# Key and value projections as seven block products instead of eight, with rotation and splitting moved into attention

## Chip, cores and metric

One core of a Trainium2 chip. The metric is the device time of one execution in microseconds, lower is better. Kernels are compared by runs on the same chip.

## What is computed

Two layers of a gated cross-attention model over 8 sequences of 256 tokens (2048 tokens in all, 1024 features), all in float32:

```
x = x + tanh(g_xattn[0]) * autocorrelation(layernorm(x), ctx, ctx)
x = x + tanh(g_ffn[0])   * lora_ffn(layernorm(x))
x = x + tanh(g_xattn[1]) * gqa_attention(layernorm(x), ctx, ctx, mask, wq, wk, wv, wo)
x = x + tanh(g_ffn[1])   * fourier_ffn(layernorm(x))
```

The change is about the keys and values of the third line: `k = rope(ctx @ wk)` and `v = ctx @ wv`, both 2048x1024 by 1024x1024, with 8 heads of 128 for the 32 query heads. `rope` turns each head: `x*cos + rot*sin`, where `rot` exchanges the two halves of the 128 dimensions.

## The kernel before

Each large product is done as three products of parts: a float32 matrix is split into a high part (a copy rounded to fp32r, on ScalarE) and a low part (the rest, a subtraction on VectorE or GpSimd), and `three` (L147 to L152) adds high x high, high x low and low x high into one PSUM bank. So every matmul needs both parts of both operands in SBUF.

The stages run in a chain on each engine, in an order that is written out by hand: each stage has one generator per engine, and `weave` (L3132) decides at which yields the next stage's pieces are put between. The stages: kv (keys and values, L194 to L528), ac (autocorrelation, L532), f0 (first FFN), qp (queries, already as seven products), at (attention, L2274), wf (factors of the last FFN's weight, spread into attention) and f1 (last FFN). Waits are semaphores by name and key (`on.wait_ge(*at(...))`); each engine works its list in order.

**kv.** The weights wv and wk are loaded, split and kept whole in SBUF. Tokens come in four blocks `tb` of 512; a block's 8 chunks of `ctxT` (128 features x 512 tokens) are split into `kv_ch`, `kv_cl`. An output tile (128x512) is 8 chunks x 3 matmuls into one bank; there are 32 tiles of values and 32 of keys. A tile of values leaves PSUM by a ScalarE copy and a VectorE subtraction, both stored to `vd[0]`, `vd[1]`; a tile of keys is turned by three VectorE products out of PSUM (L389 to L391), added and split on GpSimd (L432, L434) and stored to `kd[0]`, `kd[1]`. The last 8 tiles of values are done one by one, and `weave` puts the first pieces of ac between them: two tiles, then two pieces of ac, and so on (L3136 to L3140).

**ac's first pieces.** Piece 1 issues the loads of the tables, x and ctx. Pieces 2 and 3: `table(0)` (L690, L844), the split of the first context, `stats(0)` (L849), `normalise(0)` and the split of the first query, whose low part is on VectorE (L943). Pieces 4 and 5: the other tables and, on TensorE, the first `spectra(0)` and `odd_spectra(0)` (L579, L597). Piece 6: `correlate(0)`.

**at.** 128 steps `u`, each: transposes of the weights of step u-2, scores of step u, values of u-2, and the output product; four steps share one head group's 512 keys and values. `load_kv` (L2604) brings high and low parts of keys and values ready to use, four DMAs at every fourth step (u%4 == 2), into two buffers.

Of the kernel before, what the change touches and what calls it, by code (L numbers as in the profile page):

```python
# [162 lines left out]
def flamingo(nc, x, ctx, ctxT, mask, gates, w0T, b0, agT, bT, gb, wq, wk, wv, wo,  # L163
             w1T, b1, enc, coef, cmask, tab, four, rope, ident, out):
    es = ExitStack()
    with es:
# [5 lines left out]
        kd = [nc.dram_tensor(f"kd{i}", [G, P, T], F, kind="Internal").ap() for i in range(2)]  # L172
        w1d = nc.dram_tensor("w1d", [D, D], F, kind="Internal").ap()
        w1f = nc.dram_tensor("w1f", [7, P, 2, 4, 512], F, kind="Internal").ap()
        vd = [nc.dram_tensor(f"vd{i}", [T, D], F, kind="Internal").ap() for i in range(2)]
# [18 lines left out]
        kv_wvh = [place(f"kv_wvh{i}", 32 * i, [P, C, 512], R) for i in range(2)]  # L194
        kv_wvl = [place(f"kv_wvl{i}", 32 * i + 16, [P, C, 512], R) for i in range(2)]
        kv_ch, kv_cl = place("kv_ch", 64, [P, C, 512], R), place("kv_cl", 80, [P, C, 512], R)
        kv_oh, kv_ol = place("kv_oh", 96, [P, 4, 512], R), place("kv_ol", 104, [P, 4, 512], R)
        kv_wkh, kv_wkl = place("kv_wkh", 112, [P, C, D], R), place("kv_wkl", 144, [P, C, D], R)
        kv_rc = place("kv_rc", 176, [P, 8, 512])
        kv_t1, kv_t2 = place("kv_t1", 192, [P, 2, 512]), place("kv_t2", 196, [P, 2, 512])  # L200
        kv_rt = place("kv_rt", 200, [P, 2, 512])


        KV_OUT = [("v", 0, i) for i in range(8)]
        for tb in range(4):
            KV_OUT += [("k", tb, g) for g in range(G)]
            if tb in (1, 2):
                KV_OUT += [("v", tb, i) for i in range(8)]
        KV_OUT += [("v", 3, 2 * tt + hf) for hf in range(2) for tt in range(4)]
        KV_NO = {o: n for n, o in enumerate(KV_OUT)}  # L210
        KV_SRC = [(wv, c) for c in range(C)] + [(wk, c) for c in range(C)]

        def kv_high(i, hf):
            c = i % C
            return kv_wvh[hf][:, c, :] if i < C else kv_wkh[:, c, halves(hf)]

        def kv_low(i, hf):
            c = i % C
            return kv_wvl[hf][:, c, :] if i < C else kv_wkl[:, c, halves(hf)]

        def kv_slot(i, hf):
            return 4 + 2 * (i % 2) + hf

        def kv_bank(o):
            kind, tb, i = o
            return i if kind == "k" or tb < 3 else 4 + (i // 2) % 2

        def kv_renews(tb, c):

            return "kv_pool" if tb == 0 or c % 3 == 2 else "kv_dve"  # L230
# [3017 lines left out]
```

## Time and profile before

| | |
|---|---|
| three runs | 2989.80, 2990.52, 2991.84 us; median 2990.52 |
| profiled execution, first to last instruction | 2990.3 us (its span; no other time of it is given) |
| TensorE busy | 2959.3 us, 99% |
| VectorE, ScalarE, GpSimd busy | 2009.8, 1282.8, 1369.9 us |
| mean granted TensorE clock | 0.998 of 2.4 GHz |

The share of busy time is a mean over stages with different limits; a matmul's printed duration overlaps with the next one's, so TensorE's pace is read from the distance between starts.

### The profile page before, as it was taken

To read this page: it belongs to the slowest core of one execution; us is meant where nothing else is said; L and a number is where in the kernel's file an instruction comes from. 1 tells how busy PE (TensorE), PEld (TensorE's weight loads), DVE (VectorE), ACT (ScalarE), POOL (GpSimd) and SP (SyncE) were. 2 spreads that over 40 slices of the span, in tenths; PEclk is the share of its full clock that TensorE was granted. 3 is DMA by queue.
4 is the path that set the end of the run, shared out by engine and by line. 5 is a ranking of instruction groups with operands and counts; after the bars stand their busy time and mean duration, and the time that the engine had idled before them with its cause. 6 is when DMAs were issued, how large, how long until landed. Compare 5 with 4: busy or idle time off the path is not lost.

```text
span 2990.3 us, 41114 instructions
## 1 busy us (share of the span) xinstructions
PE 2959.3 (99%) x14701; PEld 2482.3 (83%) x14701; DVE 2009.8 (67%) x4714; ACT 1282.8 (43%) x2686; POOL 1369.9 (46%) x1105
## 2 busy tenths in 40 slices
PE   9999999999999999999999999999999999999999
PEld 7888878887788878887888888888888888888887
DVE  4432478888655686679667777666776676666566
ACT  4111366665422422232223666555555545544332
POOL 2422388886422587777776334322322211111264
PEclk9999999999999999999999999999999999999999
DMA  7332421212555564455444787676677666665531
GB/s 254 127 120 99 166 70 50 78 64 75 191 177 166 197 179 113 113 149 152 109 112 120 242 268 239 227 242 209 193 221 244 189 196 204 208 194 166 225 108 76
DMA packets 320661, 488.29 MB, mean 163 GB/s; under 512 B 26236, under 2 KB 155644, under 8 KB 317644
## 3 DMA queue, kind: packets, MB, share of 16 engines
q1 hardware_dynamic: 319740, 484.23, 51.0%
q8 instruction: 118, 1.93, 0.3%
q10 hardware_dynamic: 720, 1.44, 0.1%
q14 instruction: 83, 0.68, 0.1%
HBM read 324.12 MB, written 161.48 MB: 162 GB/s over the span
## 4 chain that ended last, share of the span: by engine, by line
PE 61%; DVE 3%; DMA 0%; issue 0%; POOL 0%; ACT 0%; SPq 0%; DVEq 0%; ACTq 0%
PE PB L150 19%; PE PB L151 19%; PE PB L152 19%; PE PB L2401 4%; DVE qp_b L2150 1%; PE PB L2830 0%; DVE PB L2192 0%; DMA qp_raw<-in_wq 0%; DVE qp_r L2198 0%; DVE PB L2174 0%; DVE qp_c L2194 0%; DVE qp_r L2188 0%; DVE qp_r L2189 0%; POOL f1x L3046 0%; DMA qp_in<-xod 0%
## 5 line engine op out<-in xcount | busy, mean ns | idle before, releaser
L2567 POOL TENSOR_TENSOR at_ql<-at_qf,at_qh 128x512 fp32r<-128x512 f32 x128 | 166.2, 1299 | 833.9 <-ACT at_qh L2441 833.9
L2448 ACT ACTIVATE at_ss<-at_ss,at_sm,at_bs 128x256 f32<-128x256 f32 x512 | 301.9, 591 | 317.1 <-DVE at_sm L2528 317.1
L150 PE MATMUL PB<-at_woh,at_ah 128*128 128x512 f32 x1024 | 400.4, 391 | 0.6 <-DVE at_al L2550 0.6
L151 PE MATMUL PB<-at_wol,at_ah 128*128 128x512 f32 x1024 | 399.9, 390 | 0.0
L152 PE MATMUL PB<-at_woh,at_al 128*128 128x512 f32 x1024 | 399.5, 390 | 0.0
L2558 DVE SCALAR_TENSOR_TENSOR at_xt<-PB,gt,at_xt 128x512 f32<-128x512 f32 x256 | 192.1, 750 | 249.7 <-PE PB L152 249.5
L150 PE MATMUL PB<-qp_b,qp_a 128*128 128x512 f32 x896 | 350.2, 391 | 8.4 <-DVE qp_r L2196 3.8
L151 PE MATMUL PB<-qp_b,qp_a 128*128 128x512 f32 x896 | 349.3, 390 | 0.0
L152 PE MATMUL PB<-qp_b,qp_a 128*128 128x512 f32 x896 | 349.2, 390 | 0.0
L2220 POOL TENSOR_TENSOR qp_a<-qp_raw,qp_a 128x512 fp32r<-128x512 f32 x192 | 260.0, 1364 | 101.2 <-ACT qp_a L2112 98.5
L2112 ACT ACTIVATE qp_a<-qp_raw 128x512 fp32r<-128x512 f32 x192 | 113.5, 625 | 292.1 <-POOL qp_raw L2224 162.4
L2460 ACT ACTIVATE at_pth<-PB 128x512 fp32r<-128x512 f32 x256 | 139.2, 596 | 225.0 <-PE PB L2401 225.0
L152 PEld LDWEIGHTS PB<-at_woh,at_al 128*128 128x128 f32 x1024 | 192.3, 188 | 41.0
L150 PEld LDWEIGHTS PB<-at_woh,at_ah 128*128 128x128 f32 x1024 | 192.7, 188 | 37.5 <-ACT at_ah L2471 0.8
L151 PEld LDWEIGHTS PB<-at_wol,at_ah 128*128 128x128 f32 x1024 | 192.7, 188 | 35.3
L150 PEld LDWEIGHTS PB<-qp_b,qp_a 128*128 128x128 f32 x896 | 168.5, 188 | 45.9 <-DVE qp_r L2196 4.9
L152 PEld LDWEIGHTS PB<-qp_b,qp_a 128*128 128x128 f32 x896 | 168.6, 188 | 35.5
L151 PEld LDWEIGHTS PB<-qp_b,qp_a 128*128 128x128 f32 x896 | 168.6, 188 | 34.6
L2544 DVE TENSOR_TENSOR at_ptl<-PB,at_pth 128x512 fp32r<-128x512 f32 x256 | 164.8, 686 | 40.5 <-ACT at_pth L2460 40.5
L2524 DVE CUSTOM_DVE_ANT_0 at_ss<-PB,at_bi 128x256 f32<-128x256 f32 x512 | 185.4, 418 | 0.2
L150 PE MATMUL PB<-at_kh,at_qh 128*128 128x256 f32 x512 | 154.8, 302 | 0.0
L2538 DVE TENSOR_SCALAR at_ss<-at_ss,at_sm 128x256 f32<-128x256 f32 x512 | 149.3, 356 | 4.5
(314 smaller groups left out, 7570.6 us busy)
## 6 DMA issues: line engine op xcount, KB each, us to landing
at_woh<-wod SPq DMA_DIRECT2D x48, 1024.0 KB, 7.4
at_wol<-wod SPq DMA_DIRECT2D x48, 1024.0 KB, 9.6
qp_raw<-in_wq SPq DMA_DIRECT2D x32, 1024.0 KB, 5.4
qd<-qp_r SPq DMA_DIRECT2D x256, 128.0 KB, 2.5
at_qf<-qd SPq DMA_DIRECT2D x128, 256.0 KB, 3.4
at_rawo<-in_wo SPq DMA_DIRECT2D x32, 512.0 KB, 5.3
wod<-at_woh SPq DMA_DIRECT2D x16, 1024.0 KB, 5.5
wod<-at_wol SPq DMA_DIRECT2D x16, 1024.0 KB, 6.3
```

Of the source, the lines that this page charges most:

```text
L150: pe.matmul(o, ah, bh, start=start, stop=False)
L151: pe.matmul(o, ah, bl, start=False, stop=False)
L152: return pe.matmul(o, al, bh, start=False, stop=stop)
L2220: pool.tensor_tensor(qp_part(pair, i, 1), qp_weight(pair, i), asf(qp_part(pair, i, 0)), ALU.subtract).then_inc(*inc("qp_pool", ("w", pair, ...
L2401: m = pe.transpose(PB[1][:, 512 * k + P * c:512 * k + P * c + P], at_ss[s][:, c, P * k:P * k + P], idt[:, :])
L2448: m = act.activation(at_ss[s][:, c, :], at_ss[s][:, c, :], ACT.Exp, bias=z[:, 4 + c:5 + c], scale=at_bs[:, qn % 2, 8 + 2 * b + c % 2:9 + 2 ...
L2460: self.act.activation(at_pth[:, k, :], BK[2 + k], ACT.Copy).then_inc(*inc("at_act", ("pt", u, k)))
L2524: dve.tensor_tensor_reduce(out=at_ss[s][:, c, :], in0=PB[0][:, L * c:L * c + L], in1=at_bi[qn % 2][:, 2 * b + c % 2, :], scale=1.0, scalar ...
L2538: dve.tensor_scalar(at_ss[s][:, c, :], at_ss[s][:, c, :], z[:, 12 + c:13 + c], None, ALU.mult).then_inc(*inc("at_dve", ("weight", u, c)))
L2544: self.dve.tensor_tensor(at_ptl[:, k, :], BK[2 + k], asf(at_pth[:, k, :]), ALU.subtract).then_inc(*inc("at_dve", ("pt", u, k)))
L2558: self.dve.scalar_tensor_tensor(out=xt, in0=BK[6 + p % 2], scalar=gt[:, 2:3], in1=xt, op0=ALU.mult, op1=ALU.add).then_inc(*inc("at_dve", ( ...
L2567: self.pool.tensor_tensor(at_ql[n % 3][:, :], at_qf[n % 2][:, :], asf(at_qh[n % 3][:, :]), ALU.subtract).then_inc(*inc("at_pool", ("q", n)))
```

## The change

1. **Seven products in place of eight.** The job is cut into four passes: values of the first 1024 tokens, keys of the first 1024, keys of the last 1024, values of the last 1024. In each pass the 1024x1024 by 1024x1024 product is taken as 2x2 blocks of 512, and Winograd's form gives it in seven block products `n`, in the order of `KV_SEQ`. A block product is 4 tiles x 4 chunks x 3 matmuls. The seven left factors are a11, S2, S3, S1, a12, a22, S4 and the right ones b11, T2, T3, T1, b21, T4, b22 (keys swap the sides for TensorE); S1 to S4 and T1 to T4 are sums of blocks, made chunk by chunk (128x512).
2. **Operands.** Blocks are loaded again for each pass. Each chunk of each factor is split into a ring of 10 slots a side, six chunks ahead of TensorE: highs on ScalarE, lows of b (and of a's chunk 3) on VectorE, lows of a's chunks 0 to 2 on GpSimd. S1, S2, S4 are on GpSimd, S3 and all T on VectorE.
3. **Banks.** A product goes chunk by chunk over four banks, products alternating between the two sets of four; the last two go tile by tile over two banks, and ac's pieces are put between those and the product before them.
4. **Leaving PSUM.** Sums of products are formed on VectorE (ScalarE for products 0 and 2 of a pass, one GpSimd addition after product 3), and one float32 copy of keys and of values is stored, keys not turned.
5. **Attention.** `load_kv` brings keys straight and with halves exchanged, and values, in float32. GpSimd multiplies by cosine and sine (`turn_k`, at u%4 == 2), VectorE joins (`join_k`, u%4 == 3), ScalarE and GpSimd split keys and values (u%4 == 3), for the group that begins at the next step.

ac's buffers move to other addresses, and its first loads wait for the blocks that lay there (`kv_spent`).

```diff
-        KV_OUT = [("v", 0, i) for i in range(8)]
...
+        KV_SEQ = (0, 4, 3, 1, 6, 2, 5)
+        KV_PASSES = (("v", 0), ("k", 0), ("k", 1), ("v", 1))
+        KV_N = 7 * len(KV_PASSES)
+        KV_RING = 10
...
+        def kv_low(side, c):
+            return "kv_dve" if side == "b" or c == 3 else "kv_pool"
+
+        def kv_bank(n, t):
+            return 4 + t % 2 if n >= KV_N - 2 else 4 * (n % 2) + t
...
+        def kv_schedule(do):
+            do.begin()
+            for q in range(6):
+                do.prepare(q // 4, q % 4)
+            for n in range(KV_N):
+                do.product(n)
+                for t in range(4):
+                    if 4 * n + 6 + t < 4 * KV_N:
+                        do.prepare(n + 1 + (2 + t) // 4, (2 + t) % 4)
+                    do.tile(n, t)
+                    do.leave(n, t)
+                    do.load(n, t)
+                    if n >= KV_N - 2 and t % 2 and (n, t) != (KV_N - 1, 3):
+                        yield
+                if KV_N - 5 < n < KV_N - 2:
+                    yield
...
+        class KvTensor(Keys):
...
+            def chunk(self, n, t, c):
+                on, ts = self.on, slice(P * t, P * t + P)
+                for side in ("a", "b"):
+                    on.wait_ge(*at("kv_act", (side, n, c)))
+                    on.wait_ge(*at(kv_low(side, c), (side, n, c)))
...
+        class KvScalar(Keys):
...
+            def prepare(self, n, c):
...
+                    if 4 * n + c >= KV_RING:
+                        on.wait_ge(*at(*kv_chunk_done(4 * n + c - KV_RING)))
+                    self.act.activation(kv_part(side, n, c, 0), kv_factor(side, n, c), ACT.Copy).then_inc(*inc("kv_act", (side, n, c)))
...
+        class KvVector(Keys):
...
+            def prepare(self, n, c):
+                dve, on, p, k = self.dve, self.on, n // 7, n % 7
+                if n == 2:
+                    self.first_sums(0, c)
+                self.low("b", n, c)
+                if kv_low("a", c) == "kv_dve":
+                    self.low("a", n, c)
+                if k == 1 and p:
+                    self.first_sums(p, c)
...
+                if k == 2:
+                    on.wait_ge(*at(*kv_loaded("b22", p, c)))
...
+                    dve.tensor_tensor(b11, b22, t1, ALU.subtract).then_inc(*inc("kv_dve", ("T2", p, c)))
...
+            def leave(self, n, t):
...
+                if k in (0, 2):
                     return
...
+                if k == 5:
+                    dve.tensor_tensor(f, f, bank, ALU.add)
+                    m = dve.tensor_tensor(u, u, bank, ALU.add)
...
+        class KvGpsimd(Keys):
...
+            def prepare(self, n, c):
...
+                if n == 2:
+                    self.first_sum(0, c)
+                if kv_low("a", c) == "kv_pool":
...
+                    pool.tensor_tensor(kv_part("a", n, c, 1), kv_factor("a", n, c), asf(kv_part("a", n, c, 0)), ALU.subtract).then_inc(
+                        *inc("kv_pool", ("a", n, c)))
+                if k == 1 and p:
+                    self.first_sum(p, c)
...
+        class KvSync(Keys):
...
+            def begin(self):
+                for c in range(4):
+                    self.fetch("b11", 0, c)
+                for c in range(4):
+                    self.fetch("a12", 0, c)
+                    self.fetch("b21", 0, c)
+                for c in range(4):
+                    self.fetch("b12", 0, c)
+                    self.fetch("a21", 0, c)
+                    self.fetch("a22", 0, c)
+                for c in range(4):
+                    self.fetch("b22", 0, c)
...
             for u in range(NU + 5):
...
+                n = u // 4 + 1
+                if u % 4 == 3 and n < NG:
+                    do.join_k(n)
+                    do.split_k(n)
...
+                if u % 4 == 2 and n < NG:
+                    do.turn_k(n)
...
+                if u % 4 == 3 and n < NG:
+                    do.split_v(n)
                 do.split_wo(u)
...
+            def join_k(self, n):
+                dve, on, kr, ks = self.dve, self.on, at_kr[n % 2], at_ks[n % 2]
+                on.wait_ge(*at("at_pool", ("sine", n)))
+                dve.tensor_tensor(kr[0:64, :, :], kr[0:64, :, :], ks[0:64, :, :], ALU.subtract).then_inc(*inc("at_dve", ("turned", n, 0)))
+                dve.tensor_tensor(kr[64:P, :, :], kr[64:P, :, :], ks[64:P, :, :], ALU.add).then_inc(*inc("at_dve", ("turned", n, 1)))
...
+            def turn_k(self, n):
...
+                on.wait_ge(*at(f"at_k{n % 2}", ("swapped", n, 1)))
+                pool.tensor_tensor(kr[:, :, :], kr[:, :, :], c, ALU.mult).then_inc(*inc("at_pool", ("cosine", n)))
+                pool.tensor_tensor(ks[:, :, :], ks[:, :, :], s, ALU.mult).then_inc(*inc("at_pool", ("sine", n)))
...
             next(kv)
             next(ac)
-            for beside in (2, 2, 1):
-                next(kv)
-                next(kv)
-                for _ in range(beside):
-                    next(ac)
+            next(kv)
+            next(ac)
+            next(ac)
+            next(kv)
+            next(ac)
+            next(ac)
+            next(kv)
+            next(kv)
+            next(ac)
             for _ in kv:
                 pass
```

## Rows read from the trace of the kernel before

**Rows 1.** The page, part 1: busy time, share, instructions.
```profile
PE 2959.3 (99%) x14701; PEld 2482.3 (83%) x14701; DVE 2009.8 (67%) x4714; ACT 1282.8 (43%) x2686; POOL 1369.9 (46%) x1105
```
**Rows 2.** Windows of the kv stage: busy of each engine, PEclk, DMA share, GB/s.
```profile
0.00:10.00 10.00, 7.39 (x18) 3.86 (x18) 3.14 (x4) 4.36 (x7) 3.34 (x7) 1.00 0.77 238
10.00:20.00 10.00, 9.97 (x44) 8.25 (x45) 5.44 (x8) 6.45 (x12) 4.11 (x4) 1.00 0.85 282
...
50.00:60.00 10.00, 10.00 (x46) 8.29 (x45) 4.74 (x7) 2.40 (x4) 0.81 (x1) 1.00 1.01 356
...
20.00:312.00 292.00, 292.00 (x1290) 241.80 (x1289) 108.24 (x158) 62.96 (x103) 91.21 (x71) 1.00 0.40 140
```
**Rows 3.** Groups by line and shape, 0 to 367 us: busy, mean ns, idle before.
```profile
L150 PE MATMUL PB<-kv_ch,kv_wkh 128*128 128x512 f32 x256 | 99.6, 389 | 0.0
...
L432 POOL TENSOR_TENSOR kv_t<-kv_t,kv_t 128x512 f32<-128x512 f32 x32 | 41.3, 1290 | 103.9 <-DVE kv_t L391 103.9
...
L330 ACT ACTIVATE kv_oh<-kv_t 128x512 fp32r<-128x512 f32 x32 | 20.2, 632 | 137.6 <-POOL kv_t L432 137.6
...
L404 DVE TENSOR_TENSOR kv_wkl<-kv_rc,kv_wkh 128x512 fp32r<-128x512 f32 x16 | 10.9, 693 | 8.3 <-ACT kv_wkh L350 8.2
```
**Rows 4.** Timeline of PE, one tile of values: start, duration; 24 matmuls apart.
```profile
312.10 0.39 PE L150 MATMUL PB<-kv_wvh,kv_ch 128*128 128x512 f32 x1
...
317.54 0.39 PE L150 MATMUL PB<-kv_wvh,kv_ch 128*128 128x512 f32 x1
```
**Rows 5.** Timeline of the first microseconds, POOL and PE.
```profile
6.44 1.29 POOL L441 TENSOR_TENSOR kv_cl<-kv_rc,kv_ch 128x512 fp32r<-128x512 f32 x1 [5.20 <-ACT kv_ch L346]
...
7.03 2.06 PE L298 MATMUL PB<-kv_wvh,kv_ch 128*128 128x512 f32 x8 [1.30 <-ACT kv_wvh L350]
```
**Rows 6.** L2194 by operands (ns min/median/max), then timeline of DVE and POOL, queries.
```profile
L2194 DVE TENSOR_TENSOR PB<-PB,qp_rope x54: 698/699/700, 1061.4 to 1611.0; 128x512 f32<-128x512 f32 x54
L2194 DVE TENSOR_TENSOR qp_c<-qp_c,qp_rope x10: 691/1638/1661, 1071.4 to 1755.1; 128x512 f32<-128x512 f32 x10
...
1067.06 1.29 DVE L2174 TENSOR_TENSOR PB<-qp_c,PB 128x512 f32<-128x512 f32 x2
...
1069.57 1.80 DVE L2192 TENSOR_TENSOR PB<-qp_c,qp_rope 128x512 f32<-128x512 f32 x1
1071.41 1.65 DVE L2194 TENSOR_TENSOR qp_c<-qp_c,qp_rope 128x512 f32<-128x512 f32 x1
...
1073.58 1.18 DVE L2198 TENSOR_TENSOR qp_r<-qp_r,qp_c 128x512 f32<-128x512 f32 x1
...
1069.52 2.99 POOL L2220 TENSOR_TENSOR qp_a<-qp_raw,qp_a 128x512 fp32r<-128x512 f32 x2
...
1075.87 1.28 POOL L2220 TENSOR_TENSOR qp_a<-qp_raw,qp_a 128x512 fp32r<-128x512 f32 x1
```
**Rows 7.** Timeline at the handover to ac: DVE, ACT, PE.
```profile
324.55 0.96 DVE L847 TENSOR_TENSOR ac_tl<-ac_tr,ac_th 128x768 fp32r<-128x768 f32 x1
...
334.52 1.23 DVE L943 TENSOR_TENSOR ac_ql<-ac_xn,ac_qh 128x1024 fp32r<-128x1024 f32 x1 [6.18 <-ACT ac_qh L710]
...
336.86 2.95 DVE L847 TENSOR_TENSOR ac_tl<-ac_tr,ac_th 128x1024 fp32r<-128x1024 f32 x3
...
326.57 1.06 ACT L718 ACTIVATE ac_ch<-ac_cb 128x1024 fp32r<-128x1024 f32 x1 [2.06 <-DMA ac_cb<-in_ctx]
...
333.86 0.39 PE L150 MATMUL PB<-ac_ch,ac_th 128*128 128x512 f32 x1
```
**Rows 8.** Timeline of two attention steps, PE and ACT; landing times of the keys.
```profile
1805.95 0.36 PE L150 MATMUL PB<-at_kh,at_qh 128*128 128x256 f32 x1
...
1815.09 0.36 PE L150 MATMUL PB<-at_kh,at_qh 128*128 128x256 f32 x1
...
1820.82 0.61 ACT L2441 ACTIVATE at_qh<-at_qf 128x512 fp32r<-128x512 f32 x1
...
DMA to landing us min/median/max: 3.7/4.6/9.6
```

More of the change, by code:

```diff
@@ L211, in flamingo @@
[L211 to L226, printed above, removed]
@@ new lines, in kv_emptied, with kv_chunk_done @@
+        def kv_emptied(n, t):
+            return ("kv_act" if n % 7 in (0, 2) else "kv_dve", ("out", n, t))
+        def kv_chunk_done(q):
+            return ("kv_pe", ("out", q // 4, 3) if q % 4 == 3 else ("chunk", q // 4, q % 4))
+        def kv_schedule(do):
[14 more added lines that the diff above has]
+                    yield
@@ new lines, in flamingo, with none, __init__, claim @@
+        class Keys:
+            def none(self, *args):
+                pass
+            begin = prepare = product = tile = leave = load = none
+        class KvTensor(Keys):
+            def __init__(self, pe, on, spare):
+                self.pe, self.on, self.spare = pe, on, spare
+            def claim(self, n, t):
+                for e in self.spare[kv_bank(n, t)]:
+                    self.on.wait_ge(*at(*e))
+                self.spare[kv_bank(n, t)] = [kv_emptied(n, t)]
+            def begin(self):
+                self.on.wait_ge(*at("kv_pool", "zeros"))
+                for _ in range(3):
+                    self.pe.matmul(BK[0], kv_st[0][:, 0:P], kv_st[0][:, :], start=True, stop=True)
+            def chunk(self, n, t, c):
[3 more added lines that the diff above has]
+                    on.wait_ge(*at(kv_low(side, c), (side, n, c)))
+                rows, cols = ("a", "b") if KV_PASSES[n // 7][0] == "v" else ("b", "a")
+                m = three(self.pe, BK[kv_bank(n, t)], (kv_part(rows, n, c, 0)[:, ts], kv_part(rows, n, c, 1)[:, ts]),
+                          (kv_part(cols, n, c, 0), kv_part(cols, n, c, 1)), c == 0, c == 3)
+                if c == 3:
+                    m.then_inc(*inc("kv_pe", ("out", n, t)))
+                elif t == 3:
+                    m.then_inc(*inc("kv_pe", ("chunk", n, c)))
+            def product(self, n):
+                if n < KV_N - 2:
+                    for c in range(4):
+                        for t in range(4):
+                            if c == 0:
+                                self.claim(n, t)
+                            self.chunk(n, t, c)
+            def tile(self, n, t):
+                if n > KV_N - 3:
+                    self.claim(n, t)
+                    for c in range(4):
+                        self.chunk(n, t, c)
@@ new lines, in flamingo, with kv_spent @@
+        VALUES_DONE = (KV_N - 1, 3)
+        def kv_all_kept(on):
+            for t in range(4):
+                on.wait_ge(*at(f"kv_s{t}", (len(KV_PASSES) - 1, 6)))
+        def kv_spent(on, name):
+            n = KV_N - 7 + {"a11": 3, "b11": 3, "a12": 4, "b22": 4, "a21": 5, "b12": 5, "a22": 6, "b21": 6, "s1": 2, "t1": 2}[name]
+            side = "a" if name in ("s1", "a11", "a12", "a21", "a22") else "b"
+            on.wait_ge(*at("kv_act", (side, n, 3)))
+            for c in (2, 3):
+                on.wait_ge(*at(kv_low(side, c), (side, n, c)))
@@ L2317, in at_schedule @@
                 do.bias(0, part)
+            do.turn_k(0)
             yield
+            do.join_k(0)
             for n in range(2):
```

548 lines of the change are left out of this document (233 added, 315 removed).

## The prediction

> **What bounds the kernel now.** I read the page first: TensorE is busy 99% of the span, no other engine over 67% [rows 1]. So matmuls taken away shorten the run, unless something else then sets the pace of the stage they leave. The windows put that to the stage: from 20 to 312 us TensorE is busy for all of the 292 us, with VectorE busy 37% of it, GpSimd 31%, ScalarE 22%, the clock at 1.00 [rows 2]. The kv stage is bound by TensorE and by nothing else; only its first 10 us have gaps. The groups by line give prices, with the matmul's printed 389 ns overlapping the next one [rows 3]; the distance between starts is the pace: 5.44 us for 24 matmuls of 512 columns, 0.2267 us each [rows 4].
>
> **What goes.** Before: 64 tiles x 8 chunks x 3 = 1536 matmuls, 348.2 us. After: 28 products x 4 tiles x 4 chunks x 3 = 1344, 304.7 us. The shape is the same, so **43.5 us** go. A product is 48 matmuls, 10.9 us; a pass of seven 76.2 us. What VectorE, ScalarE and GpSimd did for the turned keys and the splits of the results goes too, and costs nothing, since it lay under TensorE.
>
> **What comes in the kv stage.** Per pass, in instructions on 128x512 [prices: rows 3]:
> - ScalarE: 56 highs and 8 copies out of PSUM, 64 x 0.63 = 40 us of 76. Hidden.
> - GpSimd: 21 lows, 12 sums, 4 additions: 37 x 1.29 = 48 us.
> - VectorE: 35 lows and 20 sums with both inputs in SBUF, 24 additions with one input in PSUM. Two in a row take 1.29 us, so 0.60 each [rows 6]: 33 + 14.4 = 47 us.
> - DMA: 8 MB in and 4 MB out in 76 us, some 165 GB/s, where 356 have run [rows 2]. SyncE's loads for the next pass wait for the last split of the block they overwrite and stand behind stores that wait for VectorE, but come one to four products (11 to 44 us) before their use. Hidden, but for the start.
>
> Each alone has room. But VectorE and GpSimd get in each other's way: the same line takes 699 ns at most with an input in PSUM, and 1638 in the median with both in SBUF while GpSimd works [rows 6]. Four GpSimd operations (1069.52 to 1075.87, 6.35 us) let three such VectorE ones through, so one GpSimd operation holds the inputs' way for (6.35 - 3 x 0.60) / 4 = 1.13 us. A pass needs 37 x 1.13 + 55 x 0.60 = **74.8 us** of it, 1.4 less than TensorE's 76.2. The 24 additions out of PSUM fit beside GpSimd's work or add up to 14.4 us: between 74.8 and 89.2.
>
> By product, what is prepared in the seven steps of a pass takes 14.5, 13.3, 11.1, 12.1, 6.4, 6.4 and 11.1 us of this, against 10.9 us each. Four heavy steps run late by about 7 us together, two light ones make it up. Preparation is six chunks ahead (16 us of TensorE) and VectorE's first heavy step has no PSUM addition that holds it back, so walking the queue by these prices TensorE is kept fed, by some 3 us. I take 2 us lost in each of the last three passes, **6** (bounds 0, and 3 x 13 = 39 where no addition finds cover).
>
> The Trainium skill, page "SBUF — State Buffer", section "Who interferes with whom", speaks against the change here: a VectorE instruction with two SBUF inputs and a GpSimd one share a port, and the one that comes second blocks for the first one's whole instruction. With the whole printed lengths a pass would need 37 x 1.29 + 55 x 0.69 = 86 us of the port, 10 over TensorE. The blocking is as the trace shows it; the length is not, since a GpSimd operation and a VectorE one got through in 1.73 us together, not in 1.98.
>
> **The first pass.** TensorE now waits for both lows of chunk 0: GpSimd's ends at 7.7 where TensorE began at 7.03 [rows 5]: 0.7. Product 2 needs S1, T1 and, behind them in VectorE's list, T2, which waits for b22, the last of 32 loads. Its chunk 0 is load 29, 7.6 MB. After 10 us 2.4 MB are in; at 282 to 356 GB/s the rest takes 15 to 18 [rows 2], so VectorE stands until 25 to 28. Then each chunk needs four VectorE operations, a ScalarE copy and three GpSimd ones, 5 us and up to 6.4 in strict turn (4 x 0.60 + 0.63 + 3 x 1.13), and TensorE takes 2.7. It wants the last chunk of product 2 at 37.7 and gets it at about 40 to 44. I take 4 there, 2 more for product 3, with the 0.7 **7** (3 to 11).
>
> **The handover to ac.** Before, 10.9 us of kv tiles lay between the place of pieces 2 and 3 and `spectra(0)`; now two tiles of 2.72, 5.4 us. VectorE's chain there, `table(0)` at 324.55 to the first query's low part at 335.75, took 11.2 us, of which some 2 were a late load of the context (ScalarE waited 2.06 for it); the low part was ready 0.8 us before TensorE wanted it, 12 matmuls into `spectra(0)` [rows 7]. After: VectorE comes to `table(0)` behind the additions of product 25, the last of which waits for that product's end E, so at E + 0.7 to 3; the query is ready at E + 10 to 14, TensorE wants it at E + 8.2: 2 to 6 lost. Then VectorE has three lows and four additions (7 x 0.60) ahead of `table(1)` (1.2 of the 2.95 for tables 1 to 3), which TensorE wants 2.7 later: 2.7 more. I take **7** (4 to 9). ScalarE and GpSimd have less to do there.
>
> **Attention.** Per four steps (36.6 us): ScalarE 2 x 0.63, VectorE 2 x 0.69, GpSimd 4 x 1.29, one load of 0.25 MB fewer. The chain that counts is at u%4 == 3: scores at 1815.09, exponentials done at 1820.82, 5.73 later; then the split of keys, 0.63 on ScalarE and 1.29 on GpSimd, 7.7; the next scores come 9.14 after the last [rows 8]. So 1.4 us are left, if GpSimd is free. `turn_k` waits for the loads (4.6 us in the median, 9.6 at most) a step earlier; the latest would push it into VectorE's queue. `join_k` sits in a gap before the next PSUM addition. I take **3** for all 31 groups and for the pieces put into the end of the queries (bounds 0, and 31 x 2 = 62).
>
> **Sum.** 2990.3 - 43.5 + 7 + 6 + 7 + 3 = **2970 us**. The span read stands 0.2 below the median of the runs, so nothing is added. Own range 2958 to 2980. Less than 0.2%, 6 us, counts as no change.
>
> **Rivals.**
> - **Nothing new waits** (0.17): the queues hide all but the start and half of the handover. 2990.3 - 43.5 + 3 + 4 = 2951. For it: every engine has room on average. Against: the handover's chain stands in the trace and its cover is halved.
> - **The shared port sets the pace of the passes, partly** (0.16): half the PSUM additions find no cover, 82 us a pass, 4 x 5.8 = 23 lost in the passes: 2990.3 - 43.5 + 23 + 1 + 7 + 3 = 2981, and up to 2990 at 84.4 us a pass. For it: 98% use of the port by two queues that each wait in order.
> - **It sets the pace fully, slower** (0.06): no addition is covered, 89.2 a pass, 52 lost; 2990 - 43.5 + 52 + 1 + 7 + 3 = 3010. It decides from 84.5 us a pass on, where less than a third of the additions is covered. Against it: the 1.13 us measured and that GpSimd, when the port is short, always has something to do beside an addition. By the rule of the Trainium skill's page "SBUF — State Buffer" quoted above, with whole lengths and full cover, the time would be 2996.
> - **Attention waits for keys, slower** (0.05): GpSimd's four operations come in the way of the weight factors' ones and VectorE's join waits for them; 2 us for each of 31 groups, 3029. It decides from 1 us a group on. Against: the 1.4 us of room.
>
> That it does not do what it says is out: the loops give 1344 matmuls. Forecast 0.56. Faster by over 0.2%: forecast, first rival and half of the second, 0.81; within 0.2%: the rest of the second and a little of the slow ones, 0.09; slower 0.10. The range 2952 to 2988 leaves out the two slow cases and parts of the fast one and the port's.
>
> **What would show it.** TensorE's kv matmuls 1344, at 0.2267 apart in the passes; a few us of idle in 30 to 55 us behind lows and sums; passes 76 to 79 us apart; VectorE subtractions well over 0.69 in the mean; two gaps in `spectra(0)` of 2 to 6 us, ended by VectorE; scores of every fourth step without a wait. Wrong if passes are 82 us or more apart, if the first scores of a group wait for `at_kl`, or if no gap shows at the handover.

## Result: 3038.5 us, 1.6% slower, and the profile after

The changed kernel takes **3038.47 us** (median of 4 runs, 3035.38 to 3041.25), the kernel before 2990.66 beside it: ratio 1.0158, 95% interval 1.0143 to 1.0172. The forecast was 2970, the range 2952 to 2988. The profiled execution took 3041.25 us, its span is 3039.3.

The page of the changed kernel, busy time, share and instructions, answers to [rows 1]:

```profile
PE 2950.1 (97%) x14509; PEld 2465.5 (81%) x14509; DVE 2264.7 (75%) x4916; ACT 1381.3 (45%) x2878; POOL 1675.7 (55%) x1303
```

TensorE has 89 us of gaps now where it had 31. Where they opened is read from five starts on TensorE in both traces:

| start of | before | after | difference |
|---|---|---|---|
| first transposes of ac | 376.09 | 369.24 | -6.9 |
| scores of attention's step 0 | 1617.02 | 1614.75 | -2.3 |
| scores of step 36 | 1943.05 | 1976.74 | +33.7 |
| scores of step 124 | 2747.37 | 2796.57 | +49.2 |
| end of the span | 2990.3 | 3039.3 | +49.0 |

So two things went wrong, of different weight. Of the 43.5 us of matmuls taken away, 36.6 were given back by the first transposes of ac; and attention lost 51.5 from its step 0 on, of which 36.0 in its first 36 steps. Another 4.6 went between the first transposes and step 0, most of it in one wait of 3.4 for the first group's keys (`at_kl` below), which are turned, joined and split at the end of the queries.

What TensorE waited for, the view of waits (total us, times, longest) of the changed kernel:

```profile
PE PB L150 <- POOL at_wol L2635: 17.5, 8, 2.8
PE PB L2426 <- DVE at_ss L2580: 14.9, 14, 2.0
PE PB L150 <- DVE kv_st L397: 7.6, 5, 2.4
PE PB L150 <- DVE ac_ql L954: 5.5, 1, 5.5
...
PE PB L150 <- DVE kv_a L345: 4.1, 1, 4.1
PE PB L150 <- POOL at_kl L2622: 3.4, 1, 3.4
```

The two largest are attention's, and neither is by name a wait for keys: the low part of wo, split by GpSimd, and the weights, scaled by VectorE.

**The kv stage and the handover.** TensorE's timeline, rows with a wait and the first ones behind the wait at 44:

```profile
44.28 0.77 PE L150 MATMUL PB<-kv_b,kv_a 128*128 128x512 f32 x1 [4.07 <-DVE kv_a L345]
44.84 0.63 PE L151 MATMUL PB<-kv_b,kv_a 128*128 128x512 f32 x1
45.27 0.63 PE L152 MATMUL PB<-kv_b,kv_a 128*128 128x512 f32 x1
...
49.42 0.39 PE L150 MATMUL PB<-kv_b,kv_a 128*128 128x512 f32 x1
...
133.13 0.50 PE L150 MATMUL PB<-kv_a,kv_b 128*128 128x512 f32 x1 [2.40 <-DVE kv_st L397]
...
292.27 0.79 PE L150 MATMUL PB<-kv_b,kv_a 128*128 128x512 f32 x1 [2.39 <-DVE kv_st L397]
...
322.93 0.47 PE L150 MATMUL PB<-ac_ch,ac_th 128*128 128x512 f32 x1 [2.30 <-DVE ac_tl L858]
...
331.44 0.77 PE L150 MATMUL PB<-ac_qh,ac_th 128*128 128x512 f32 x1 [5.50 <-DVE ac_ql L954]
```

A pause can cost more than its length: behind the 4.07 us matmuls start 0.43 apart instead of 0.2267 until 49.42. The windows of the same stretch show the granted clock (the number behind POOL's busy time): 0.66 in the ten us of the pause, 1.00 ahead of it.

```profile
30.00:40.00 10.00, 10.00 (x46) 8.11 (x44) 9.90 (x9) 1.69 (x3) 8.72 (x6) 1.00 0.02 9
40.00:50.00 10.00, 5.93 (x16) 4.57 (x16) 9.90 (x10) 7.95 (x18) 9.31 (x6) 0.66 0.12 45
```

Summing every distance between starts above 0.2267 gives the bill with the half clock in it: some 3 us at the start (first matmul at 8.54 instead of 7.03), 8.6 between 40 and 54, then 5.1, 1.3 and 6.4 in the three later passes, 11.9 between 320 and 339. Some 11 us of it are half clock, by the distances behind the pauses.

Not every pause has it behind it. The pause of 2.40 at 133.13 cost 4.3 us here; in the run called weights first below, with the same kv code and the same pause (at 133.29), it cost 2.7, without any half clock. In the eight traces of this kv code (the change, kv alone, no turn, turn last, keys early, one join, weights first, two moves) the first transposes begin between 366.6 and 372.4 us: the waits are alike there, the half clock is not.

Why the bank is late, in VectorE's and GpSimd's rows of the same pause:

```profile
129.04 0.67 DVE L397 TENSOR_TENSOR kv_st<-kv_c,PB 128x512 f32<-128x512 f32 x1
129.64 1.17 DVE L345 TENSOR_TENSOR kv_b<-kv_b,kv_b 128x512 fp32r<-128x512 f32 x1
130.73 1.75 DVE L380 TENSOR_TENSOR kv_b<-kv_b,kv_b 128x512 f32<-128x512 f32 x1
132.41 0.68 DVE L397 TENSOR_TENSOR kv_st<-kv_c,PB 128x512 f32<-128x512 f32 x1
...
135.78 0.68 DVE L345 TENSOR_TENSOR kv_b<-kv_b,kv_b 128x512 fp32r<-128x512 f32 x1
...
130.21 5.10 POOL L438 TENSOR_TENSOR kv_a<-kv_a,kv_a 128x512 fp32r<-128x512 f32 x3
```

Beside GpSimd a low and a sum take 1.17 and 1.75 us, and one tile's addition comes 3.37 behind the last; TensorE makes a tile in 2.72. When GpSimd has stopped, at 135.31, the same low takes 0.68.

**Attention, first kind of wait.** The timeline of one group in the first quarter, SyncE's queue, GpSimd and TensorE:

```profile
1793.96 0.46 SPq L2676 DMA_DIRECT2D at_kr<-kd  x1
1794.47 1.12 SPq L2678 DMA_DIRECT2D at_ks<-kd  x2
...
1798.77 1.29 POOL L2609 TENSOR_TENSOR at_ql<-at_qf,at_qh 128x512 fp32r<-128x512 f32 x1 [5.32 <-ACT at_qh L2467]
1801.00 1.28 POOL L2617 TENSOR_TENSOR at_kr<-at_kr,qp_rope 128x512 f32<-128x512 f32 x1 [0.93 <-DMA at_ks<-kd]
1802.24 1.29 POOL L2618 TENSOR_TENSOR at_ks<-at_ks,qp_rope 128x512 f32<-128x512 f32 x1
1803.49 2.34 POOL L2635 TENSOR_TENSOR at_wol<-at_rawo,at_woh 128x1024 fp32r<-128x1024 f32 x1
...
1805.97 0.47 PE L150 MATMUL PB<-at_woh,at_ah 128*128 128x512 f32 x1 [2.80 <-POOL at_wol L2635]
```

`turn_k` stands ahead of `split_wo` in GpSimd's list. TensorE wants the low part at 1805.97 - 2.80 = 1803.17. In the step before, 9.14 us earlier, the split had ended at 1793.46, which is 1802.60 one step on: 0.6 us of room. The wait of 0.93 for the swapped keys and 2.5 us for the two products put it 2.8 behind. Without the wait for keys it is 1.9, as in three of the eight groups (1.85 to 1.87).

**Second kind.** VectorE's four weight factors (L2580), a step without keys and one with them, and GpSimd beside the latter:

```profile
1788.55 1.14 DVE L2580 TENSOR_SCALAR at_ss<-at_ss,at_sm 128x256 f32<-128x256 f32 x4
...
1846.21 0.47 PE L150 MATMUL PB<-at_woh,at_ah 128*128 128x512 f32 x1 [1.86 <-POOL at_wol L2635]
1849.25 0.75 DVE L2600 SCALAR_TENSOR_TENSOR at_xt<-PB,gt,at_xt 128x512 f32<-128x512 f32 x1 [1.12 <-PE PB L152]
1849.17 1.29 POOL L2622 TENSOR_TENSOR at_kl<-at_kr,at_kh 128x512 fp32r<-128x512 f32 x1 [3.11 <-ACT at_kh L2471]
1850.12 5.48 DVE L2580 TENSOR_SCALAR at_ss<-at_ss,at_sm 128x256 f32<-128x256 f32 x4
1850.44 1.35 POOL L2609 TENSOR_TENSOR at_ql<-at_qf,at_qh 128x512 fp32r<-128x512 f32 x1
1851.81 1.29 POOL L2627 TENSOR_TENSOR at_vl<-at_vr,at_vh 128x512 fp32r<-128x512 f32 x1
1853.06 2.39 POOL L2635 TENSOR_TENSOR at_wol<-at_rawo,at_woh 128x1024 fp32r<-128x1024 f32 x1
...
1855.65 0.77 PE L2426 MATMUL PB<-idt,at_ss 128*128 128x128 f32 x5 [2.02 <-DVE at_ss L2580]
```

Four factors take 5.48 us instead of 1.14, as long as GpSimd's four operations beside them: each waits for one. In an ordinary step the factors are all but done when GpSimd begins (1789.63); here VectorE comes to them 2.1 us later in its step than in that one, and GpSimd, which begins with the split of the keys, is first.

Of the 31 groups whose keys are turned between steps 9 are caught like this, for different reasons. In four of the first quarter, this one among them, VectorE stood waiting for TensorE's output product (row at 1849.25, 1.12 us), because TensorE had itself just waited for wo (row at 1846.21, 1.86): the second kind follows from the first. The join alone puts the factors back by 0.2 us, which costs nothing in 17 groups; with a piece of the bias (0.69 us) in the same gap as well two groups, at 2151 and 2450, lose 1.9 us each. A ninth costs 0.4. And in two groups the keys are late:

```profile
2601.85 1.29 POOL L2617 TENSOR_TENSOR at_kr<-at_kr,qp_rope 128x512 f32<-128x512 f32 x1 [4.95 <-DMA at_ks<-kd]
2604.43 0.68 DVE L2570 TENSOR_TENSOR at_kr<-at_kr,at_ks 64x512 f32<-64x512 f32 x1 [2.77 <-POOL at_ks L2618]
```

GpSimd waits 4.95 us for the load (3.44 in the other group), VectorE 2.77 for GpSimd (1.26), and the factors behind the join are late. These two cost 11.4 of the 15.5 us lost behind step 36. Why these loads land late was not asked.

### The profile page after: what moved, and what is told of

It reads as the page before. It is cut to its first block, busy times and chain, and to the rows that moved or that the text cites. A ratio compares the mean times of both kernels' runs of the same rounds, so it can differ in the third digit from the quotient of the medians.

```text
span 3039.3 us, 41663 instructions
## 1 busy us (share of the span) xinstructions
PE 2950.1 (97%) x14509; PEld 2465.5 (81%) x14509; DVE 2264.7 (75%) x4916; ACT 1381.3 (45%) x2878; POOL 1675.7 (55%) x1303
## 4 chain that ended last, share of the span: by engine, by line
PE 54%; DVE 5%; POOL 2%; DMA 2%; ACT 1%; issue 0%; SPq 0%; DVEq 0%; POOLq 0%; ACTq 0%
PE PB L150 17%; PE PB L151 17%; PE PB L152 17%; PE PB L2426 3%; DMA at_ks<-kd 1%; DVE at_ss L2580 1%; POOL at_wol L2635 1%; DVE qp_b L2159 1%; DMA qp_raw<-in_wq 0%; PE PB L2892 0%; POOL at_kr L2617 0%; POOL at_ks L2618 0%; DVE PB L2201 0%; DVE at_ptl L2586 0%; ACT at_ss L2483 0%
## 5 line engine op out<-in xcount | busy, mean ns | idle before, releaser
L2483 ACT ACTIVATE at_ss<-at_ss,at_sm,at_bs 128x256 f32<-128x256 f32 x512 | 301.9, 591 | 326.0 <-DVE at_sm L2563 326.0
L2580 DVE TENSOR_SCALAR at_ss<-at_ss,at_sm 128x256 f32<-128x256 f32 x512 | 181.8, 419 | 4.5
```

Source lines behind the costliest of these rows:

```text
L2483: m = act.activation(at_ss[s][:, c, :], at_ss[s][:, c, :], ACT.Exp, bias=z[:, 4 + c:5 + c], scale=at_bs[:, qn % 2, 8 + 2 * b + c % 2:9 + 2 ...
L2580: dve.tensor_scalar(at_ss[s][:, c, :], at_ss[s][:, c, :], z[:, 12 + c:13 + c], None, ALU.mult).then_inc(*inc("at_dve", ("weight", u, c)))
```

## Experiments

Theories: **A**, attention's loss is order in GpSimd's list; **B**, late loads of keys; **C**, the shared port by the sum of GpSimd's work, whatever the order; **D**, added later, weight factors caught between GpSimd's operations; **E** and **F**, banks emptied late by order, or the port, in kv; **G** and **H**, the handover. In the first experiment A and B are wider: A is attention's turning and splitting, B what kv leaves behind, or the clock. The starts of scores give attention's loss apart from the rest (before: 326.0 us from step 0 to step 36, 804.3 from there to step 124):

| run | time, us | ratio to before | steps 0-36 | steps 36-124 |
|---|---|---|---|---|
| the change | 3038.5 | 1.0158 | +36.0 | +15.5 |
| kv alone | 2984.5 | 0.9981 | +0.2 | 0.0 |
| no turn | 2988.7 | 0.9996 | 0.0 | 0.0 |
| turn last | 3026.5 | 1.0126 | +25.3 | +19.3 |
| keys early | 3020.8 | 1.0105 | +28.8 | +9.3 |
| one join | 3013.0 | 1.0071 | +21.9 | +4.9 |
| weights first | 2999.6 | 1.0028 | +11.2 | +2.6 |
| two moves | 3006.7 | 1.0053 | +11.1 | +6.7 |
| last version | 2987.8 | 0.9990 | +5.4 | +1.4 |

The times are medians, the last two columns of the one execution that was profiled. In turn last that is the slowest of four (3021.6 to 3034.2), in the last version the fastest of eleven (2982.6 to 2992.7).

**kv alone.**

```diff
-                    on.wait_ge(*at("at_act", ("k", n)))
-                    on.wait_ge(*at("at_pool", ("k", n)))
+                    on.wait_ge(*at(f"at_k{n % 2}", ("low", n)))
...
+                sp.dma_start(asf(at_kh[s][:, :]), kd[g][:, rows]).then_inc(*landed(f"at_k{s}", ("high", n)))
+                sp.dma_start(asf(at_kl[s][:, :]), kd[g][:, rows]).then_inc(*landed(f"at_k{s}", ("low", n)))
```

> The kv stage as after the change, attention as before it: keys and values are loaded twice and neither turned nor split, so the keys' rotation and both splits are left out. Theory A (the loss sits in attention's turning and splitting, the kv part gains what the first transposes of ac show, 376.09 before and 369.24 after, 7 us): 2983 to 2988 us, first transposes at 369, steps of attention 36.56 us a group throughout. Rival B (the loss in attention has to do with what kv leaves behind, or with the clock in general): 3020 or more, with pauses in attention as after the change.

2984.46 us, 0.9981 (0.9972 to 0.9990). First transposes at 370.1, attention as before to 0.2 us. The kv part is worth some 6 us; all else is attention's turning and splitting. Theory A's number, not B's, in the sense of this run: it does not yet part order in a list from late loads.

**No turn.** `turn_k` and `join_k` leave the schedule, and in both splits:

```diff
-                self.on.wait_ge(*at("at_dve", ("turned", n, 1)))
+                self.on.wait_ge(*at(f"at_k{n % 2}", ("swapped", n, 1)))
```

> Keys are not turned: GpSimd's two products and VectorE's two half additions per group are left out, loads and splits stay. Theory A: the wait for wo's low part goes as with the turn behind it, and VectorE's weight factors are no longer pushed into GpSimd's splits, so nearly all of the 49 us lost in attention go: 2990 to 3000 us. Rival C (the port, by GpSimd's total): two of four operations are gone, so half of the loss, 3012 to 3018 us.

2988.66, 0.9996 (0.9986 to 1.0005), better than either theory said. The four splits of keys and values that stay cost attention nothing, though they are half of GpSimd's new work: against C. The loads stand where the change has them, so late keys alone cost nothing either, only by way of the turn and the join.

**Turn last.**

```diff
-                if u % 4 == 2 and n < NG:
-                    do.turn_k(n)
...
                 do.split_wo(u)
+                if u % 4 == 2 and n < NG:
+                    do.turn_k(n)
```

> One move: GpSimd turns the keys behind the split of wo of the same step instead of ahead of it. Theory A (in the first quarter GpSimd's two products of the turn stand ahead of the wo low part that TensorE is about to read, 1.9 to 2.8 us late in eight groups, and 2 us more each at half clock): those pauses go, 25 to 32 us, 3006 to 3013 us. Rival B (the swapped keys land late, and whoever waits for them is late whatever the order): 3030 to 3045, with the pause moved to the keys' low part or to the weights. Rival C (the shared port: 2.5 us more of GpSimd's work block VectorE wherever they stand): 3025 to 3040.

3026.47, 1.0126 (1.0104 to 1.0149): 12 us of the 25 to 32 that A expected. Between 1660 and 2800 us the view of waits has a single line left:

```profile
PE PB L2426 <- DVE at_ss L2580: 25.1, 24, 2.0
```

The wait for wo is gone entirely, so A holds for it. The weights take its place, 25.1 us in 24 waits for 14.9 in 14. A alone is not enough, and theory D was formed from this.

**Keys early.**

```diff
-        at_ks = [place(f"at_ks{i}", kb + 4, [P, 2, L]) for i, kb in enumerate((76, 20))]
+        at_ks = [place(f"at_ks{i}", kb, [P, 2, L]) for i, kb in enumerate((76, 20))]
...
+                if u % 4 == (2 if n == 1 else 1) and n < NG:
+                    do.turn_k(n)
+                if u % 4 == (3 if n == 1 else 2) and n < NG:
+                    do.split_k(n)
```

> Nothing left out. The swapped keys go to the place of the high part instead of that of the values, so that keys are loaded two steps earlier; GpSimd turns them at the end of the step after, VectorE joins them a step earlier, and all splits on GpSimd stand at the end of their step, behind the split of wo. Theory A (all of attention's loss is the order in GpSimd's list): 45 of 49 us go, 2990 to 2998 us, no wait for wo's low part and hardly any for the weights. Rival C (the port by GpSimd's total): 3020 to 3040. Rival B (late loads): as A here, but then the run with the turn moved alone stays at 3030 or more.

3020.78, 1.0105 (1.0090 to 1.0120), far from A's 2990 to 2998. Loads are two steps ahead, so B is out as the main cause, though late keys have the share shown above. New are a wait of 4.1 us for the second group's keys and three, 3.6 us together, for the DMA that brings wo's low part. And 13.8 us of waits for the weights stay, in 11 places. In one of them (1752.94) the two half joins and two turns of a query by VectorE stand in a gap of some 1.1 us, and the factors begin 1.8 us later in their step than in the one before, beside GpSimd.

**One join.**

```diff
+                dve.scalar_tensor_tensor(kr[:, :, :], ks[:, :, :], at_sign[:, :], kr[:, :, :], op0=ALU.mult, op1=ALU.add).then_inc(
+                    *inc("at_dve", ("turned", n, 1)))
```

> As the run with the keys loaded early, and VectorE joins the two halves in one instruction on 128 partitions (the sine part times a column of plus and minus one, plus the cosine part) instead of two on 64. Theory D (what is left in attention is VectorE coming to its four weight factors later than GpSimd comes to its splits, after which each factor waits for one GpSimd operation, 4.9 us for four instead of 1.1): the join takes 0.7 us instead of 1.4 of a gap of 1.1, so the factors are late in fewer steps; half of the remaining 32 us go, 3000 to 3010 us. Rival C (the port by the sum of GpSimd's work, whatever the order): 3015 to 3021.

3012.99, 1.0071 (1.0056 to 1.0086). A join of 0.75 us instead of two of 0.68: 8 us for 0.6 us less in VectorE's list, and waits for the weights in 7 places, not 11. As D, a little less than it said.

**Weights first.** The test of D itself: one wait.

```diff
                 self.on.wait_ge(*at("at_act", ("q", n)))
+                if n > 2:
+                    self.on.wait_ge(*at("at_dve", ("weight", n - 3, 3)))
```

> As the run with the single join, and GpSimd's split of a query waits until VectorE has written the last weight factor of the step before. Theory D: no weight factor waits for GpSimd any more, four of them take 1.1 to 1.5 us throughout and the waits of the transposes for them go; what is left is GpSimd up to 1 us later with the low part of wo in some steps of the first quarter. 2988 to 3000 us. Rival C: as without the wait or slower, 3005 to 3025.

2999.62, 1.0028 (1.0018 to 1.0038): 13 us faster by making GpSimd wait. The factors in the changed kernel (min/median/max ns), then in this run:

```profile
L2580 DVE TENSOR_SCALAR at_ss<-at_ss,at_sm x512: 339/349/2429, 1626.0 to 2838.8; 128x256 f32<-128x256 f32 x171
```

```profile
L2586 DVE TENSOR_SCALAR at_ss<-at_ss,at_sm x512: 344/349/357, 1618.3 to 2794.0; 128x256 f32<-128x256 f32 x171
```

No factor is held any more, and TensorE never waits for them. GpSimd does the same work on the same tiles, so C is out and D shown. What is left are four waits for GpSimd's low part of wo (3.4 us), three for the DMA that brings it (1.7), one of 1.6 for the first group's keys and one of 4.1 us for the second group's, which this run splits at the end of the step before.

**Two moves.** As turn last, and in GpSimd's `split_k`:

```diff
+                if n:
+                    self.on.wait_ge(*at("at_dve", ("weight", 4 * n - 2, 3)))
```

> Two orders and nothing else: the turn of the keys behind the split of wo, and GpSimd's split of the keys waits until VectorE has written the last weight factor of the step before. Keys are loaded where the change loads them, the join is in two instructions. Theory D (in the run with the turn moved alone the weight factors, caught between GpSimd's splits, took the place of the wait for wo): 15 to 25 us of the 36 left go, 3000 to 3012 us; what is left is keys and wo's low parts that GpSimd now reaches 1 to 2 us later. Rival C (the port by the sum of GpSimd's work): 3022 to 3030.

3006.66, 1.0053 (1.0040 to 1.0067), in D's range. Two orders in one list give back 32 of the 48 us. Of the 6.7 us still lost behind step 36, 6.2 stand at three groups whose swapped keys GpSimd waits 5.83, 3.99 and 3.69 us for: that is B's share, with the loads where the change has them.

**Small sums, in kv.** Six sums on one column:

```diff
-                    dve.tensor_tensor(b12, b22, b12, ALU.subtract).then_inc(*inc("kv_dve", ("T3", p, c)))
+                    dve.tensor_tensor(b12[:, 0:1], b22[:, 0:1], b12[:, 0:1], ALU.subtract).then_inc(*inc("kv_dve", ("T3", p, c)))
```

> Attention as after the change; in kv six of the eight sums of a pass run on one column instead of 512, so the sums are left out but for one column, and lows, highs, additions, waits and loads stay as they are. The port is asked for 18.6 us less a pass (56 instead of 75). Theory F (the pauses of kv are the port's: VectorE comes late to its additions out of PSUM because its lows and sums alternate with GpSimd's operations): 21 us of pauses and half clock between 40 and 300 us go but for 0 to 4, first transposes of ac at 348 to 355 instead of 369. Rival (order and loads, not the port): 364 to 370.

First transposes at 346.1, 23 us earlier, a little more than F expected. The stretch from 20 to 290 us of this run, then 20 to 300 of the changed kernel (busy PE, PEld, DVE, ACT, POOL, then the clock):

```profile
20.00:290.00 270.00, 270.00 (x1193) 223.65 (x1192) 202.89 (x286) 126.66 (x236) 172.09 (x137) 1.00 0.50 163
```

```profile
20.00:300.00 280.00, 267.48 (x1140) 217.64 (x1139) 260.98 (x275) 127.39 (x234) 218.14 (x131) 0.97 0.45 149
```

TensorE has no gap at all, with every load, copy, addition and low in place. So the pauses in the passes come of what VectorE and GpSimd have to do there, and not of loads or order. The run takes VectorE's own time away too (four sums, 9.6 us a pass by 0.60 each) and does not part it from the port. The lengths do: without holds VectorE's 79 operations of a pass would fill 47 us of 76, and at 129 to 136 the same low takes 1.17 us beside GpSimd and 0.68 alone. Theory F. Of the 23 us, 1.6 are half clock at the start, which this execution did not have.

**Additions together, and additions first.** In the first run the four additions of a product move ahead of the next chunks in every list, in the second in VectorE's alone (by a list of chunks put off until the fourth addition).

```diff
                 do.product(n)
+                if n < KV_N - 2:
+                    for t in range(4):
+                        do.leave(n, t)
                 for t in range(4):
...
-                    do.leave(n, t)
+                    if n >= KV_N - 2:
+                        do.leave(n, t)
```

> Attention as after the change; in kv the four additions of a product out of PSUM stand together ahead of the next product's chunks in every list instead of one behind each chunk. Theory E (the pauses at 129, 234 and 289 us are banks emptied late, behind lows and sums in VectorE's list): they go with their half-clock stretches, 12.9 us, and the 1.9 at 51; first transposes of ac at 355 to 359 instead of 369. Rival F (the port is short in the passes, so that lows are late if additions are not): same loss at other places, 366 to 372.

> Attention as after the change; in kv only VectorE's list is changed: the four additions of a product out of PSUM come ahead of the last three of the four chunks that it prepares beside it, ScalarE and GpSimd as after the change. Theory E (banks emptied late by the order of VectorE's list, with slack in the lows): the pauses at 129 and 289 us shrink from 5 to 6 us each to 2 or less, first transposes at 358 to 363. Theory F (the port): the same loss returns as waits for lows, 365 to 375.

Transposes at 403.5 and 374.4, against 369.2. Waits for lows and for ScalarE's highs came in the place of the waits for banks (14.4 us for `kv_b` in the first run and 17.1 put down to no engine; 5.4 for `kv_a` and 3.1 for `kv_b` in the second). In the first, ScalarE's copies of chunks were held too, so it says little of VectorE; the second says that order is not what is short. E is out.

**Handover, two tiles more; statistics early.** The first moves two tiles of product 26 ahead of the first spectra:

```diff
             next(ac)
             next(kv)
             next(ac)
-            next(ac)
             next(kv)
             next(ac)
+            next(kv)
             next(ac)
-            next(kv)
+            next(ac)
             next(kv)
             next(ac)
```

The second has VectorE do the statistics of x in its gap ahead of product 25's additions:

```diff
             def leave(self, n, t):
+                if (n, t) == (KV_N - 3, 0):
+                    KV_HOOK["stats"]()
...
             table(0)
             yield
-            stats(0)
```

> Attention as after the change; two more tiles of kv (5.4 us) stand between the handover's table and the first spectra of ac. Theory G (the 2.3 and 5.5 us before the first spectra are VectorE's and ScalarE's chain of table, statistics and first query, which starts with the last product's lows): 5.4 us of it are covered and with it the half clock, so 11.9 shrink to 2 to 5, first transposes at 360 to 363 instead of 369. Rival: the chain starts later by as much, because VectorE's additions of these two tiles come ahead of its work for ac: 368 to 372.

> Attention as after the change; at the handover VectorE computes the statistics of the first block of x in the gap ahead of the additions of product 25, not behind the table's low part, and GpSimd finishes them ahead of the context's low part. Theory H (the 5.5 us for the first query's low part are the chain statistics, GpSimd's four small operations, normalising, high and low part, which starts only when VectorE is through with kv and the table): that wait goes, the one for the table stays at 2 to 3.5; with the half clock 6 to 9 of 11.9 us go, first transposes of ac at 360 to 364 instead of 369. Rival (kv's own last additions and lows hold VectorE back, whatever stands behind them): 367 to 371.

Two tiles more: transposes at 372.8, no gain. VectorE's additions of these tiles come ahead of the statistics, which start at 329.15 instead of 322.75: the rival was right. Of TensorE's waits those for the table and the query shrink to 0.5 and 1.1 us, but one of 5.1 us for VectorE's addition `kv_u` is new, and one of 3.6 for ScalarE's high part of a context. Statistics early: the rows of TensorE at the handover,

```profile
328.01 0.47 PE L150 MATMUL PB<-ac_ch,ac_th 128*128 128x512 f32 x1 [2.71 <-DVE ac_tl L861]
335.57 0.47 PE L150 MATMUL PB<-ac_ch,ac_th 128*128 128x512 f32 x1 [0.26 <-ACT ac_kk L744]
```

show the 5.50 gone and the table's wait left, 6.0 us with the half clock for 11.9: theory H, at the low end of what it promised. The transposes, 367.0, came later than expected because the first pass and the start lost 3 us more in this execution.

**Versions with all that helped.** Weights first with the second group's keys split at once (`do.split_k(1)` behind its join), first with the sums of the first pass two chunks earlier, then without that but with the early statistics:

```diff
-                if n == 2:
-                    self.first_sums(0, c)
...
+                if (n, c) in KV_FIRST:
+                    self.first_sums(0, KV_FIRST[n, c])
```

> All that helped, nothing left out: keys loaded early, one join, weights ahead of GpSimd's splits, the second group's keys split at once, and in kv's first pass the first three sums of a chunk two chunks earlier. From the run with weights first (2999.6, its profile 2994.9) the 4 us wait of the second group's scores go, and of the 8.6 us lost at 40 to 54 us some 4: 2985 to 2993 us, the same as the kernel before or faster by 0.2%. If the first pass is the port's and not the order's, 2990 to 2996.

> Nothing left out: the early statistics with all that helped in attention (keys loaded early, one join, weights ahead of GpSimd's splits, the second group's keys split at once), kv's first pass as the change has it. From 2996.7 by 7 us at the handover and 2 to 3 in the first pass: 2983 to 2991, 0 to 0.3% faster than the kernel before. If the handover's chain is not the statistics, 2992 to 2997.

The first: 2996.69, 1.0017 (1.0008 to 1.0026); 0.7 above the range for the case that the first pass is the port's. The first pass lost 9.8 us between 37 and 57 instead of 8.6, so an earlier place for its sums does not help. The second: **2987.82**, 0.9990 (0.9981 to 0.9999) of the kernel before. It is ahead of both kernels, of the one before by 0.1%, half of what counted as a change above.

## Why the prediction was wrong

- **The step that failed** is attention's term, 3 us, which had no price for what stands behind `turn_k` in GpSimd's list nor for late weight factors; attention lost 51.5. The rest of the sum gave 20 us for what measured 36.6.
- **What goes**, 43.5 us: right. 1344 matmuls and 0.2267 us between starts where nothing waits.
- **The first pass**, 7: 8.6 between 40 and 54 and some 3 at the start, 12. The mechanism holds (chunks of product 2 every 5.7 us, priced 5 to 6.4, the wait for the last one 4.07, ended by VectorE), but half clock was in no term, here or below: 2.4 us behind the 4.07, 1.6 at the start. The start's 0.7 went by GpSimd's low part (ready at 7.84); VectorE's, which began 0.5 us later and took 1.34, ended at 8.39.
- **The three later passes**, 6: they lost 12.8. The port was seen as 74.8 of 76.2 us, and small sums with the lengths shows that it is the port; where both queues are full, a GpSimd operation and a VectorE one come every 1.69 us (GpSimd's starts 41.91, 43.59, 45.27, 46.97), as priced (1.73). The failed step is "walking the queue by these prices TensorE is kept fed, by some 3 us": it followed lows only. The waits are for `kv_st`: VectorE's low, sum and addition of one tile took 3.37 us at 129 to 133, TensorE needs 2.72, and it is the bank that is late. With the loss, half clock included, a pass comes to 80.5 us in the mean (77.5 to 82.6), where the forecast had 78.2 and whole printed lengths gave 86.
- **The handover**, 7: two gaps ended by VectorE, as foreseen, and 11.9. The query's low part was the larger term, 5.50 us where 2 to 6 stood; the table's 2.30 came ahead of the first spectra and not behind them; a third gap, 1.3, was ScalarE's; half clock made up the rest.
- **Attention**, 3: it lost 51.5, and 4.6 went ahead of it, and this decides the sign. Two sentences failed. "`turn_k` waits for the loads ... a step earlier; the latest would push it into VectorE's queue" looked at the load and at VectorE, and not at what stands behind `turn_k` in GpSimd's own list: `split_wo`, with 0.6 us of room in a step of the first quarter. The push into VectorE's queue that the same sentence names did come, in two groups and for 11.4 us, and had no price in the 3. "`join_k` sits in a gap before the next PSUM addition" put 1.4 us into a gap of 1.1, which by itself is 0.2 late and harmless, and did not ask what else fills the gap and who is late when VectorE is: the weight factors, and with GpSimd beside them a start 0.8 us late becomes an end 4 us late (in the group at 2151), and 2.1 become 6.4 (at 1843). The 1.4 us of room worked out for the keys were for the one chain that never waited but at its start: the sign "the first scores of a group wait for `at_kl`" showed once, at the first group.
- **The rivals.** "Attention waits for keys, slower", chance 0.05, 3029 us, had the right stage and sign and the right price in the mean (51.5 / 31 = 1.7 us a group), on the wrong waits: not for keys, and 4.5 us in each of the eight groups with a wait for wo, in bursts thereafter. That its 3029 is near 3038 is in part luck: it has 20 us for kv and the handover, as the forecast does. GpSimd's operations "in the way of the weight factors' ones" stood in it, and what was counted against it, the 1.4 us of room, was no argument against that. The rival in which the port sets the pace partly (82 us a pass) priced the passes better than the forecast did.
- With the 36.6 us measured in kv and at the handover instead of 20, and attention as forecast, the sum would have been 2986; kv alone measured 2984.5.

## What to carry to other kernels

When an operation is put into an engine's list, ask first what stands behind it in that list and how much room that one has in the tightest stage, here 0.6 us, and only then how long its own result may take. VectorE and GpSimd were here a queue without an order: instructions 0.8 us late found the other engine in front and then waited for its operations one by one, and a wait that held the other engine back was cheaper than the contention (13 us, for one line). A resource at 98% of the pace gave pauses. A pause can cost its length and half clock behind it (2.4 us behind 4.07, 1.7 behind 2.80, none behind 2.31 at 1681.34), and that belongs into the range.

## What the runs showed of the hardware that was not expected

- A VectorE instruction with one tile in SBUF and a scalar for each partition is held by GpSimd too: the factor on 128x256 took 349 ns in the median and 2429 at most, the length of GpSimd's split of wo (2.39 us). The prediction's sums had counted only instructions with two inputs in SBUF; a rival of it named the weight factors. The Trainium skill, page "SBUF — State Buffer", section "Who interferes with whom", lists `tensor_scalar` among the operations that can take the shared ports and says that the second to come blocks for the whole instruction of the first; the trace agrees, with 5.48 us for four factors beside four GpSimd operations.
- Half the partitions cost as much as all: the two parts of the join on 64x512 took 0.67 and 0.69 us, a sum on 128x512 in kv 0.68 where nothing held it, the single join on 128x512, with a factor, 0.75.
- Behind some pauses TensorE ran at 1.2 instead of 2.4 GHz for a while, 0.43 us between starts: 44.28 to 49.42 behind 4.07 us, and again in attention behind 2.80 us, from 1807.24 to 1810.22. Behind others it did not: 2.31 us at 1681.34, and the same 2.40 us in kv with and without it in two executions. In attention the waits of the changed kernel sum up to 32.4 us between steps 0 and 124, and 51.5 were lost.
